# Opening of a layer norm, FFN and attention kernel: batch 1 prepared from the second tile on

## The chip, the cores and the metric

One core of a Trainium2 chip runs the whole kernel. The metric is the device time of one execution in microseconds (us). The five engines run side by side and wait for one another by semaphores only: TensorE (PE, with its weight loads as PEld), VectorE (DVE), ScalarE (ACT), GpSimd (POOL), and SyncE (SP), which issues the DMAs.

## What is computed

```python
x = L0_attn_hidden_states                      # (4, 512, 1024), fp32
xn = _layernorm(x, axis=-1)
s = _L0_attn_ref(xn, Wq, Wk, Wv, Wo)           # 16 heads, rotary, causal
g = _silu(_L0_ffn_ref(xn, ...))
x = x + s * g
...
router_logits = xf @ gate_w.T                  # _L0_ffn_ref, xf = xn as (2048, 1024)
routing = jax.nn.softmax(router_logits, axis=1)        # 8 experts
in_scale = routing @ in_channel_scale
out_scale = routing @ out_channel_scale
out = xf * in_scale @ jnp.sign(weight).T * out_scale + bias
```

## The kernel before

The tokens are 16 tiles of 128 rows, four to each of four batches. The FFN block runs first over all batches (the first 215 us or so), then the attention block. The order of work on each engine is written out by hand; nothing is scheduled by a program. Every fp32 matrix product is made of a high part (`hi`, rounded) and a low part (`lo`, the rest).

The preparation of batch r+1 runs between the FFN matmuls of batch r:

- DVE: `layer_norm(n)` = `ln_stats(n, 2)` (statistics of tiles n and n+1) and `ln_finish(n, 2)` (five small operations after ACT's square root `ln_root`, then the normalisation of both tiles).
- PE: `x_transposes(n)` turns tile n; ACT: `x_high(n)` copies it out in four pieces (hi, and the full value, for two halves); DVE: `x_low(n)` makes the low part. For the tiles of batch 1 and later, `x_transposes(n)` waits for the low parts of tile n-1, since both pass through the same PSUM banks `ff_tr`.
- PE `gate`, ACT `gate_copy`, PE `gate_transposes`, ACT `parts_copy`, DVE `router` with `route_exp` on ACT in its middle, PE `route_transposes`, ACT `route_copy`: the softmax over the experts.
- For each of the eight slices k of 128 channels: PE `in_scale` (one matmul into `ff_tr`), DVE `scale` (writes `xs_full`, two buffers), ACT `xs_high`, POOL `xs_low` (L688). `scale(k)` waits for `xs_low(k-2)`.
- PE `ffn(n, ks)`: four matmuls a slice; at slices 0 and 4 one more for the output scale, which ACT copies (`out_scale`). DVE `z_scale(n)` multiplies, POOL `z_bias(n)` adds the bias.

For batches 1 to 3 the four tiles of batch r+1 are transposed at points spread from the end of `ffn(4r)` to the first slice of `ffn(4r+2)`. For batch 0 the code has a sequence of its own (`if j == 0`), shown with its neighbours here:

Of the kernel before, what the change touches and what calls it, by code (L numbers as in the profile page):

```python
# [21 lines left out]
WARM = (6, 4, 3, 6)  # L22
# [35 lines left out]
def ffn_block(nc, block, io, keep, xn, xn_store, z_store):  # L58

    with ExitStack() as ctx:  # L60
# [147 lines left out]
        def _(pe):  # L208
# [108 lines left out]
            ffn(1, range(KT))  # L317
            for j in range(BATCH):
                more = j + 1 < BATCH
                m = QT * (j + 1)  # L320
                if j == 0:
                    x_transposes(m)
                    ffn(2, range(1))
                    x_transposes(m + 1)
                    ffn(2, range(1, 4))
                    x_transposes(m + 2)
                    ffn(2, range(4, 6))
                    x_transposes(m + 3)
                    ffn(2, range(6, KT))
                    gate(1)  # L330
                    ffn(3, range(2))
                    gate_transposes(1)
                    ffn(3, range(2, 4))
                else:
# [7 lines left out]
                    ffn(QT * j + 1, range(4))  # L342
                    if more:
                        x_transposes(m + 1)
                    ffn(QT * j + 1, range(4, KT))
                    if more:
                        x_transposes(m + 2)
                    ffn(QT * j + 2, range(1))
                    if more:
                        x_transposes(m + 3)  # L350
                    ffn(QT * j + 2, range(1, 4))
                    if more:
                        gate(j + 1)
                    ffn(QT * j + 2, range(4, 6))
                    if more:
                        gate_transposes(j + 1)
                    ffn(QT * j + 2, range(6, KT))
                    ffn(QT * j + 3, range(4))
# [8 lines left out]
        def _(act):  # L367
# [81 lines left out]
            parts_copy(0)  # L449
            route_exp(0)  # L450
            sign(4)
            chan_high(1)
            route_copy(0)
            xs_high(0, range(1))
            xs_high(0, range(1, 2))
            out_scale(0, 0)
            sign(5)
            xs_high(0, range(2, 3))
            sign(6)
            xs_high(0, range(3, 4))  # L460
            sign(7)
            xs_high(0, range(4, KT))
            ln_root(2, 2)
            out_scale(0, 1)
            out_scale(1, 0)
            out_scale(1, 1)
            for j in range(BATCH):
# [3 lines left out]
                if j == 0:  # L471
                    x_high(m)
                    out_scale(2, 0)
                    x_high(m + 1)
                    ln_root(3, 2)
                    out_scale(2, 1)
                    x_high(m + 2)
                    x_high(m + 3)
                    ln_root(4, 2)
                    gate_copy(1)  # L480
                    out_scale(3, 0)
                    parts_copy(1)
                    route_exp(1)
                    out_scale(3, 1)
                    route_copy(1)
                    xs_high(1, range(4))
                    continue
                out_scale(n, 0)
# [38 lines left out]
        def _(dve):  # L527
# [117 lines left out]
            for j in range(BATCH):  # L645
# [17 lines left out]
                if more:  # L663
                    x_low(m)
# [838 lines left out]
```

In the opening ACT also takes the signs of the eight weight rows (`sign(t)`) and copies the two channel tables (`chan_high(c)`; DVE makes their low parts in `chan_low(c)`). `warm(count)` issues matmuls whose result nobody reads.

## Time and profile before

| what | value |
|---|---|
| three runs | 1182.59, 1185.58, 1187.51 us (median 1185.58) |
| profiled execution | 1184.56 us, span 1182.8 us |
| PE busy | 1140.3 us, 96% of the span |
| DVE, ACT, POOL busy | 721.6, 610.7, 420.0 us |
| granted TensorE clock, mean | 0.991 |

The profile shows one execution. Its span is 1.8 us shorter than its time. Times in its views are counted from the start of the span. Busy shares are means over the FFN and the attention, which have different limits, so the change has to be read from the first 90 us.

### The profile page before, as it was taken

The numbers are of one execution on the slowest core, as the hardware profiler recorded it, in microseconds if no ns is written. First come the engines' busy times: TensorE is split into PE (matmuls) and PEld (weight loads), VectorE is DVE, ScalarE is ACT, GpSimd is POOL, SyncE is SP. The second block draws the span as 40 slices with busy tenths as digits, with TensorE's granted clock in tenths as the row PEclk, the third lists the DMA queues.
The fourth block names the chain that finished last, engine by engine and source line by source line (L and its number), as shares of the span: only waits on it lengthen the run. The fifth ranks groups of instructions, "written<-read, shape, count | busy, mean of one in ns | idle before, by whom it ended". The sixth has DMA issues, their size and how long they took to land.

```text
span 1182.8 us, 17759 instructions
## 1 busy us (share of the span) xinstructions
PE 1140.3 (96%) x5699; PEld 949.4 (80%) x5699; DVE 721.6 (61%) x1732; ACT 610.7 (52%) x1285; POOL 420.0 (36%) x253
## 2 busy tenths in 40 slices
PE   5879999999999999999999999999999997999998
PEld 4657777788888888888888888888888886888886
DVE  6466453267776776777776776777776777333132
ACT  6445443155665656646665566655665666322211
POOL 0415527452423533334334242352423533221220
PEclk9889999999999999999999999999999999999999
DMA  9425132302202012022360220202202115555653
GB/s 370 181 89 206 50 118 84 95 7 66 62 9 62 34 46 62 9 66 61 148 213 9 71 62 9 62 13 67 62 9 62 38 60 187 168 178 187 204 176 125
DMA packets 87270, 112.00 MB, mean 95 GB/s; under 512 B 3408, under 2 KB 68944, under 8 KB 86224
## 3 DMA queue, kind: packets, MB, share of 16 engines
q1 hardware_dynamic: 87248, 111.72, 28.7%
q8 instruction: 12, 0.20, 0.1%
q14 instruction: 10, 0.08, 0.0%
HBM read 78.15 MB, written 33.55 MB: 94 GB/s over the span
## 4 chain that ended last, share of the span: by engine, by line
PE 86%; DVE 6%; ACT 4%; POOL 2%; issue 1%; DMA 0%; SPq 0%; DVEq 0%; ACTq 0%; POOLq 0%
PE at_proj L44 17%; PE at_proj L46 17%; PE at_proj L45 17%; PE at_out L987 7%; PE at_pt L974 6%; PE ff_z_ps L287 5%; PE at_score L956 4%; PE at_score L957 3%; PE at_score L44 2%; PE at_score L45 2%; PE at_score L46 2%; POOL ff_xs_lo L688 2%; PE at_proj L941 1%; DVE ff_stats L547 1%; DVE xs_full L609 1%
## 5 line engine op out<-in xcount | busy, mean ns | idle before, releaser
L44 PE MATMUL at_proj<-xn_hi,w_hi 128*128 128x512 f32 x896 | 362.0, 404 | 3.2 <-ACT at_v_t L1092 2.9
L46 PE MATMUL at_proj<-xn_hi,w_lo 128*128 128x512 f32 x896 | 351.0, 392 | 0.0
L45 PE MATMUL at_proj<-xn_lo,w_hi 128*128 128x512 f32 x896 | 349.5, 390 | 0.0
L46 PEld LDWEIGHTS at_proj<-xn_hi,w_lo 128*128 128x128 f32 x896 | 168.2, 188 | 37.3
L44 PEld LDWEIGHTS at_proj<-xn_hi,w_hi 128*128 128x128 f32 x896 | 168.6, 188 | 33.7 <-issue 3.3
L45 PEld LDWEIGHTS at_proj<-xn_lo,w_hi 128*128 128x128 f32 x896 | 169.0, 189 | 30.2
L1351 POOL TENSOR_TENSOR at_turning<-at_turning,rope_table 128x512 f32<-128x512 f32 x64 | 83.0, 1297 | 302.4 <-DVE at_turning L1222 302.4
L1359 POOL TENSOR_TENSOR w_lo<-w_stage,w_hi 128x1024 fp32r<-128x1024 f32 x45 | 114.5, 2558 | 162.7 <-ACT w_hi L1071 162.7
L1109 ACT ACTIVATE at_prob<-at_score,at_neg_max 128x512 f32<-128x512 f32 (+3 forms) x256 | 133.2, 526 | 69.4 <-DVE at_neg_max L1250 69.0
L1118 ACT ACTIVATE at_pt_hi<-at_pt 128x512 fp32r<-128x512 f32 (+1 forms) x192 | 94.1, 524 | 101.8 <-PE at_pt L974 101.0
L1267 DVE TENSOR_TENSOR at_pt_lo<-at_pt,at_pt_hi 128x512 fp32r<-128x512 f32 (+1 forms) x192 | 112.0, 597 | 44.2 <-ACT at_pt_hi L1118 43.2
L1250 DVE CUSTOM_DVE_ANT_0 at_score<-at_score,at_causal 128x512 f32<-128x512 f32 (+3 forms) x256 | 120.7, 514 | 1.0
L974 PE MATMUL at_pt<-ident,at_prob 128*128 128x128 f32 x640 | 93.3, 277 | 5.6 <-DVE at_pt_lo L1267 3.5
L1125 ACT ACTIVATE at_low_half<-at_out 64x512 f32<-64x512 f32 x64 | 37.9, 592 | 103.4 <-PE at_out L987 102.6
L1260 DVE TENSOR_SCALAR at_prob<-at_prob,at_inv_sum 128x256 f32<-128x256 f32 (+3 forms) x256 | 84.5, 393 | 2.3
L287 PE MATMUL ff_z_ps<-sign_t,ff_xs_hi 128*128 128x512 f32 x256 | 84.1, 410 | 1.5 <-POOL ff_xs_lo L688 1.4
L1355 POOL TENSOR_TENSOR at_rotated<-at_turning 128x512 f32<-128x512 f32 x64 | 82.9, 1295 | 7.3 <-POOL at_turning L1351 4.5
L1084 ACT ACTIVATE at_qk<-at_rotated 64x512 fp32r<-64x512 f32 x128 | 80.3, 627 | 7.1 <-POOL at_rotated L1355 5.5
L974 PEld LDWEIGHTS at_pt<-ident,at_prob 128*128 128x128 f32 x640 | 74.5, 143 | 10.9 <-DVE at_pt_lo L1267 4.4
L1367 POOL TENSOR_TENSOR w_lo<-rope_table,w_hi 128x1024 fp32r<-128x1024 f32 x16 | 41.2, 2575 | 115.6 <-ACT w_hi L1138 115.6
L287 PE MATMUL ff_z_ps<-sign_t,ff_xs_lo 128*128 128x512 f32 x256 | 81.7, 401 | 0.0
L956 PE MATMUL at_score<-at_qk 128*128 128x512 f32 (+3 forms) x256 | 80.4, 327 | 0.0
(123 smaller groups left out, 1795.3 us busy)
## 6 DMA issues: line engine op xcount, KB each, us to landing
z_store<-z SPq DMA_DIRECT2D x16, 512.0 KB, 2.6
w_stage<-in_L_attn_Wq_dram SPq DMA_DIRECT2D x16, 512.0 KB, 3.9
w_stage<-in_L_attn_Wk_dram SPq DMA_DIRECT2D x16, 512.0 KB, 5.2
w_stage<-in_L_attn_Wv_dram SPq DMA_DIRECT2D x16, 512.0 KB, 6.2
att_store<-at_att_t SPq DMA_DIRECT2D x32, 256.0 KB, 2.0
rope_table<-att_store SPq DMA_DIRECT2D x16, 512.0 KB, 6.7
z<-_attn_hidden_states_dram SPq DMA_DIRECT2D x16, 512.0 KB, 4.7
at_turning<-z_store SPq DMA_DIRECT2D x16, 512.0 KB, 6.0
```

The source lines that it names most:

```text
L44: pe.matmul(out, sh, mh, start=first, stop=False)
L45: pe.matmul(out, sh, ml, start=False, stop=False)
L46: return pe.matmul(out, sl, mh, start=False, stop=final)
L287: last = pe.matmul(z_ps[n % 2][:, o, :], part[:, k, tok], keep["sign_t"][:, k, o * HALF:(o + 1) * HALF], start=(k == 0 and part is xs_hi), ...
L956: pe.matmul(out, q, k_hh[parity][h][:, 0:width], start=True, stop=False)
L974: last = pe.transpose(pt_ps[u % 2][:, dst:dst + P], prob[h][:, src:src + P], keep["ident"][:])
L1109: last = act.activation(prob[h][:, P_COL[t]:P_COL[t] + width], score_ps[bank][:, col:col + width], ACT.Exp, scale=-1.0, bias=neg_max[h][:, ...
L1118: act.activation(pt_hi[h][:, 512 * u:512 * u + PT_WIDTH[u]], pt_ps[u % 2][:, 0:PT_WIDTH[u]], ACT.Copy).then_inc(pt_high, 1)
L1250: last = dve.tensor_tensor_reduce(out=row, in0=row, in1=causal[:, (QT - 1 - t) * P:SEQ], scale=-1.0, scalar=FAR, op0=ALU.add, op1=ALU.min, ...
L1260: last = dve.tensor_scalar(part, part, inv_sum[h][:, t:t + 1], None, ALU.mult)
L1267: dve.tensor_tensor(pt_lo[h][:, cols], pt_ps[u % 2][:, 0:PT_WIDTH[u]], raw(pt_hi[h][:, cols]), ALU.subtract).then_inc(pt_ready, 1)
L1359: pool.tensor_tensor(w_lo[m][:], w_raw[m], raw(w_hi[m][:]), ALU.subtract).then_inc(w_ready[m], 1)
```

## The change

PE: for batch 0 the special sequence is dropped, and batch 1's first tile (tile 4) is transposed right behind `ffn(0)`, tile 5 in the middle of `ffn(1)`, tile 6 ahead of `ffn(2)` and tile 7 behind its first slice, as in later batches. Seven of 19 warm matmuls go. DVE: the statistics of tiles 4 and 5 are taken one tile at a time between scales, and their square root and normalisation come between scales too; the statistics of tiles 6 and 7 come before `z_scale(0)`. ACT: a small `exp_table()` puts the load of the exponential's table ahead of `gate_copy(0)`; `sign(0)` and `chan_high(0)` move ahead of `x_high(0)`, the other signs move by some places, `chan_high(1)` comes earlier, and `ln_root(2)` moves from behind the eighth `xs_high` to behind the fifth. `chan_low(1)` moves ahead of the scales.

```diff
@@ PE
-            warm(WARM[1])
             pe.wait_ge(tables, 1)
             gate(0, (0, 1))
             gate(0, (2, 3))
+            warm(WARM[1])
+            gate_transposes(0)
             warm(WARM[2])
-            gate_transposes(0)
-            warm(WARM[3])
...
-            ffn(1, range(KT))
             for j in range(BATCH):
...
                 if j == 0:
                     x_transposes(m)
-                    ffn(2, range(1))
-                    x_transposes(m + 1)
-                    ffn(2, range(1, 4))
-                    x_transposes(m + 2)
-                    ffn(2, range(4, 6))
-                    x_transposes(m + 3)
-                    ffn(2, range(6, KT))
-                    gate(1)
-                    ffn(3, range(2))
-                    gate_transposes(1)
-                    ffn(3, range(2, 4))
...
+                ffn(QT * j + 1, range(4))
+                if more:
+                    x_transposes(m + 1)
+                ffn(QT * j + 1, range(4, KT))
+                if more:
+                    x_transposes(m + 2)
+                ffn(QT * j + 2, range(1))
+                if more:
+                    x_transposes(m + 3)
+                ffn(QT * j + 2, range(1, 4))
@@ ACT
+            def exp_table():
+
+                act.activation(route_e[0:1, 0, 0:1], ln[0:1, 1, 0:1], ACT.Exp)
...
             ln_root(0, 2)
+            sign(0)
+            chan_high(0)
             x_high(0)
             ln_root(1, 2)
             x_high(1)
-            chan_high(0)
-            sign(0)
+            sign(1)
             x_high(2)
             x_high(3)
-            sign(1)
-            sign(2)
-            sign(3)
+            exp_table()
+            chan_high(1)
             gate_copy(0)
             parts_copy(0)
             route_exp(0)
...
+            xs_high(0, range(4, 5))
+            ln_root(2, 2)
+            xs_high(0, range(5, 6))
@@ DVE
-            ln_stats(4, 2)
-            scale(0, range(4, KT))
-            ln_finish(4, 2)
+            scale(0, range(3))
+            ln_tile(4, 0)
+            scale(0, range(3, 4))
+            ln_moments(ln_tile(4, 1), 2)
+            scale(0, range(4, 5))
+            scale(0, range(5, 6))
+            ln_inverse(2)
+            scale(0, range(6, 7))
+            ln_apply(4, 0)
+            scale(0, range(7, KT))
+            ln_apply(4, 1)
+            ln_stats(6, 2)
             z_scale(0)
```

On PE, from the last slice of `ffn(0)` on, the program before had this (L279 is the output scale's matmul, L287 the FFN's, L219 the transposes; the left-out rows are the same two L287 rows, slice by slice):

```order
L287 MATMUL ff_z_ps<-sign_t,ff_xs_hi 128x512 x2
L287 MATMUL ff_z_ps<-sign_t,ff_xs_lo 128x512 x2
L279 MATMUL ff_osc_ps<-chan_out,ff_route_t 128x512
...
L287 MATMUL ff_z_ps<-sign_t,ff_xs_lo 128x512 x2
L219 MATMUL ff_tr<-ident,w_stage 128x128 x8
L279 MATMUL ff_osc_ps<-chan_out,ff_route_t 128x512
```

The changed program has this from the same slice on:

```order
L287 MATMUL ff_z_ps<-sign_t,ff_xs_hi 128x512 x2
L287 MATMUL ff_z_ps<-sign_t,ff_xs_lo 128x512 x2
L219 MATMUL ff_tr<-ident,w_stage 128x128 x8
L279 MATMUL ff_osc_ps<-chan_out,ff_route_t 128x512
```

The eight transposes of tile 4 have moved ahead of the eight slices of `ffn(1)`.

On DVE, behind the router of batch 0, the program before had this (L609 is `scale`, L547 to L552 the statistics, L564 the normalisation, L617 `chan_low(1)`):

```order
L609 TENSOR_TENSOR xs_full<-ff_tr,xn_full 128x512 x2
L617 TENSOR_TENSOR chan_out<-z,chan_out 64x1024
L609 TENSOR_TENSOR xs_full<-ff_tr,xn_full 128x512 x2
L547 BN_STATS ff_stats<-w_stage 128x6 x4
L550 BN_AGGR ff_moments<-ff_stats 128x2 x2
L552 TENSOR_SCALAR ff_ln<-ff_moments 128x2
L609 TENSOR_TENSOR xs_full<-ff_tr,xn_full 128x512 x4
...
L564 TENSOR_SCALAR w_stage<-w_stage,ff_moments,ff_ln 128x1024 x2
L624 TENSOR_TENSOR z<-ff_z_ps,ff_out_sc 128x1024
```

The changed program has this there (L598 is `scale`, L522 to L530 the statistics, L548 the normalisation, L606 `chan_low(1)`; the rows left out are four more of the five small operations that begin with L540, and then the statistics of tiles 6 and 7):

```order
L606 TENSOR_TENSOR chan_out<-z,chan_out 64x1024
L598 TENSOR_TENSOR xs_full<-ff_tr,xn_full 128x512 x3
L522 BN_STATS ff_stats<-w_stage 128x6 x2
L598 TENSOR_TENSOR xs_full<-ff_tr,xn_full 128x512
L522 BN_STATS ff_stats<-w_stage 128x6 x2
L528 BN_AGGR ff_moments<-ff_stats 128x2 x2
L530 TENSOR_SCALAR ff_ln<-ff_moments 128x2
L598 TENSOR_TENSOR xs_full<-ff_tr,xn_full 128x512 x2
L540 RECIPROCAL ff_ln<-ff_ln 128x2
...
L598 TENSOR_TENSOR xs_full<-ff_tr,xn_full 128x512
L548 TENSOR_SCALAR w_stage<-w_stage,ff_moments,ff_ln 128x1024
L598 TENSOR_TENSOR xs_full<-ff_tr,xn_full 128x512
L548 TENSOR_SCALAR w_stage<-w_stage,ff_moments,ff_ln 128x1024
```

The two normalisations stood behind all scales and now stand around the eighth; the two table operands of `chan_low(1)` are read before the first scale.

## Rows read from the trace of the kernel before

**Rows 1.** The page: the span and the engines' busy time.

```profile
span 1182.8 us, 17759 instructions
PE 1140.3 (96%) x5699; PEld 949.4 (80%) x5699; DVE 721.6 (61%) x1732; ACT 610.7 (52%) x1285; POOL 420.0 (36%) x253
```

**Rows 2.** Windows: length; busy PE, PEld, DVE, ACT, POOL; clock, DMA share, GB/s.

```profile
30.17:86.58 56.41, 47.28 (x188) 32.76 (x188) 32.35 (x72) 24.79 (x44) 18.26 (x11) 0.88 0.36 137
86.58:131.21 44.63, 43.37 (x201) 32.19 (x202) 27.37 (x58) 21.93 (x40) 19.66 (x12) 1.00 0.39 154
131.21:175.70 44.49, 43.24 (x202) 32.05 (x200) 22.18 (x44) 21.78 (x40) 19.65 (x12) 1.00 0.27 83
66.10:71.60 5.50, 5.50 (x17) 4.61 (x18) 1.65 (x3) 2.56 (x5) 0.00 (x0) 0.51 0.31 98
```

**Rows 3.** Timeline of PE: start, duration, what, and the idle time before it.

```profile
46.04 0.73 PE L287 MATMUL ff_z_ps<-sign_t,ff_xs_hi 128*128 128x512 f32 x2
...
55.04 1.04 PE L219 MATMUL ff_tr<-ident,w_stage 128*128 128x128 f32 x8
...
66.10 1.94 PE L219 MATMUL ff_tr<-ident,x_tiles 128*128 128x128 f32 x8 [4.05 <-DVE xn_lo L578]
...
105.38 1.03 PE L219 MATMUL ff_tr<-ident,w_stage 128*128 128x128 f32 x8
...
131.21 0.39 PE L262 MATMUL ff_tr<-ff_route_t,chan_in 128*128 128x512 f32 x1
```

**Rows 4.** Timeline of DVE from 56 us to 65 us.

```profile
56.86 0.69 DVE L578 TENSOR_TENSOR xn_lo<-ff_tr,xn_hi 128x512 fp32r<-128x512 f32 x1 [7.02 <-ACT xn_full L394]
...
58.45 1.21 DVE L624 TENSOR_TENSOR z<-ff_z_ps,ff_out_sc 128x1024 f32<-128x1024 f32 x1
59.58 2.46 DVE L547 BATCH_NORM_STATS2 ff_stats<-x_tiles 128x6 f32<-128x512 f32 x4
...
62.83 0.17 DVE L557 RECIPROCAL ff_ln<-ff_ln 128x2 f32<-128x2 f32 x1 [0.27 <-ACT ff_ln L378]
...
63.82 1.53 DVE L564 TENSOR_SCALAR x_tiles<-x_tiles,ff_moments,ff_ln 128x1024 f32<-128x1024 f32 x2
```

**Rows 5.** Timelines of ACT and DVE in the first 28 us.

```profile
10.77 0.60 ACT L391 ACTIVATE xn_hi<-ff_tr 128x512 fp32r<-128x512 f32 x1 [3.11 <-PE ff_tr L219]
...
13.29 0.20 ACT L378 ACTIVATE ff_ln<-ff_ln 128x2 f32<-128x2 f32 x1 [0.46 <-DVE ff_ln L552]
...
26.04 1.28 ACT L411 ACT_TABLE_LOAD   x1
27.33 0.23 ACT L411 ACTIVATE ff_route_e<-ff_route 128x32 f32<-128x32 f32 x1
...
20.03 1.22 DVE L617 TENSOR_TENSOR chan_in<-z,chan_in 64x1024 fp32r<-64x1024 f32 x1
...
26.50 0.19 DVE L588 TENSOR_TENSOR ff_route<-ff_route,ff_route_m 128x32 f32<-128x32 f32 x1
```

**Rows 6.** DMA issues between 3.0 and 4.0 us: count, size, us to landing.

```profile
weight_rows<-in_L_ffn_weight_dram SPq DMA_DIRECT2D x1, 512.0 KB, 7.2
z<-fn_in_channel_scale_dram SPq DMA_DIRECT2D x1, 512.0 KB, 8.0
```

**Rows 7.** The chain that ended last, one slice k of the scales.

```profile
39.20 0.70 DVE xs_full L609
39.92 0.64 ACT ff_xs_hi L428
40.64 1.30 POOL ff_xs_lo L688
```

**Rows 8.** One line of POOL (ns min/median/max), and rows of the attention.

```profile
L688 POOL TENSOR_TENSOR ff_xs_lo<-xs_full,ff_xs_hi x32: 1272/1288/2135, 32.2 to 187.4; 128x512 fp32r<-128x512 f32 x32
...
301.32 1.27 DVE L1260 TENSOR_SCALAR at_prob<-at_prob,at_inv_sum 128x256 f32<-128x256 f32 x4
...
977.29 2.41 POOL L1363 TENSOR_TENSOR xn_lo<-w_stage,xn_hi 128x1024 fp32r<-128x1024 f32 x1
978.74 4.15 DVE L1260 TENSOR_SCALAR at_prob<-at_prob,at_inv_sum 128x256 f32<-128x256 f32 x4
```

More of the change, by code:

```diff
@@ L21 @@
 STEPS = 2 * 2 * PAIRS
-WARM = (6, 4, 3, 6)
+WARM = (6, 2, 4)
 MASK = -1.0e9 / 8.0
@@ L341, in _ @@
                     ffn(QT * j, range(7, KT))
[L342 to L358, printed above, removed]
+                ffn(QT * j + 1, range(4))
[8 more added lines that the diff above has]
+                ffn(QT * j + 2, range(1, 4))
+                if more:
+                    gate(j + 1)
+                ffn(QT * j + 2, range(4, 6))
+                if more:
+                    gate_transposes(j + 1)
+                ffn(QT * j + 2, range(6, KT))
+                ffn(QT * j + 3, range(4))
                 if more:
@@ L450, in _ @@
             route_exp(0)
+            sign(2)
+            sign(3)
+            route_copy(0)
+            xs_high(0, range(2))
             sign(4)
[L452 to L455, printed above, removed]
+            xs_high(0, range(2, 3))
             out_scale(0, 0)
+            xs_high(0, range(3, 4))
             sign(5)
-            xs_high(0, range(2, 3))
+            xs_high(0, range(4, 5))
+            ln_root(2, 2)
+            xs_high(0, range(5, 6))
             sign(6)
-            xs_high(0, range(3, 4))
+            xs_high(0, range(6, 7))
             sign(7)
-            xs_high(0, range(4, KT))
-            ln_root(2, 2)
+            xs_high(0, range(7, KT))
             out_scale(0, 1)
-            out_scale(1, 0)
-            out_scale(1, 1)
             for j in range(BATCH):
@@ L470, in _ @@
                 m = n + QT
[L471 to L488, printed above, removed]
-                xs_high(j, range(4, KT))
-                out_scale(n, 1)
+                if j >= 1:
+                    out_scale(n, 0)
+                    xs_high(j, range(4, KT))
+                    out_scale(n, 1)
                 if not more:
@@ L540, in gate_w_low, with ln_tile, ln_moments @@
                                   raw(keep["gate_t"][:, :, 0:EXPERTS]), ALU.subtract).then_inc(tables, 1)
-            def ln_stats(n, count):
-                for t in range(count):
-                    slot = X_SLOT[n + t]
-                    dve.wait_ge(x_in[slot], 16 * X_SLOT[:n + t + 1].count(slot))
-                    for h in range(2):
-                        last = dve.bn_stats(stats[:, t, h, :], x_tile[n + t][:, h * HALF:(h + 1) * HALF])
+            def ln_tile(n, t):
+                slot = X_SLOT[n + t]
+                dve.wait_ge(x_in[slot], 16 * X_SLOT[:n + t + 1].count(slot))
+                for h in range(2):
+                    last = dve.bn_stats(stats[:, t, h, :], x_tile[n + t][:, h * HALF:(h + 1) * HALF])
+                return last
+            def ln_moments(last, count):
                 then(last)
@@ L552, in ln_stats, with ln_inverse @@
                 dve.tensor_scalar(ln[:, 0, 0:count], moments[:, 0:count, 1], LN_EPS, None, ALU.add).then_inc(ln_var, 1)
-            def ln_finish(n, count):
+            def ln_stats(n, count):
+                for t in range(count):
+                    last = ln_tile(n, t)
+                ln_moments(last, count)
+            def ln_inverse(count):
                 roots[0] += 1
```

38 lines of the change are left out of this document (16 added, 22 removed).

## The prediction

> **What bounds the kernel now.** The page comes first [rows 1]: PE is busy for 96% of the span, so work on the other engines counts only where PE stands still for it. The second view is a table of windows, cut at the first input scale matmul of batches 0, 1, 2 and 3 (30.17, 86.58, 131.21, 175.70 us) [rows 2]. All three windows hold the same kinds of work, one batch each. The second and third last 44.63 and 44.49 us with PE busy for 43.3 and at a granted clock of 1.00. The first lasts 56.41 us at 0.88. So batch 0 costs about 11.8 us more than a batch in the settled rhythm, and that is all that a new order of its work can give back.
>
> The third view, PE's timeline, says where the 11.8 us lie [rows 3]. `ffn(0)`'s last slice starts at 46.04; until there PE follows the slower chain of the scales. Then `ffn(1)` runs without a gap, and tile 4 is transposed only at 55.04. At 66.10 PE has stood idle for 4.05 us, because the low parts of tile 5 were late. DVE's timeline says why [rows 4]: DVE was idle for 7.02 us until 56.86, waiting for tile 4 to come out of PE, and then had `z_scale(1)`, the statistics of tiles 6 and 7 (2.46 us), their five small operations and their normalisation (1.53 us) in front of tile 5's low part. DVE had nothing to do, then too much. Behind PE's idle time the granted clock is 0.51 for 5.5 us [rows 2], the lower of its two levels (1.2 of 2.4 GHz), so the PE work there took twice its time: some 2.7 us more. Idle time and low clock together are 6.8 of the 11.8 us; small waits and the scales' pace in `ffn(0)` are the rest.
>
> **The change, part by part.** I follow it along the path.
>
> *Before the router.* `sign(0)` and `chan_high(0)` now stand ahead of `x_high(0)`, and their data must have landed. The weight row is issued at 3.07 us and needs 7.2, the table at 3.56 and needs 8.0 [rows 6]: 10.3 and 11.6 us. The table's copy takes 0.95, so `x_high(0)` begins at 12.57 instead of 10.77 [rows 5]. Its four copies take 1.93, so the root of tiles 2 and 3 starts at 14.50 instead of 13.29: DVE is 1.2 us late with their normalisation. Against this stand two things that leave the path: the 1.22 us of `chan_low(0)` between low parts [rows 5], and the idle time on ACT. Carried through (DVE 0.6 us for each half's low part, ACT 0.48 for each copy, transposes of tile 3 behind tile 1's low part), the last low part ends at 22.7, about 0.1 us later than before. I count a loss of 0.1.
>
> *The exponential's table.* The load stood between the router's sum and its exponential: it ran from 26.04 to 27.33 [rows 5], while DVE had the operand ready at 26.69 (26.50 + 0.19) [rows 5]. Now the exponential starts 0.6 us earlier. The load itself falls into the time between tile 3's last copy (about 21.8) and `gate_copy(0)` (24.8), where ACT needs 1.28 + 0.2 + 0.95 for the load, the dummy and `chan_high(1)` and ends at 24.25; were that cover gone, up to 1.3 us would be back. The trace shows the exponential right behind the load, so 0.6 is all of it. The Trainium skill, ScalarE: Activation LUTs, What ACT_TABLE_LOAD costs, adds a drain of about 1.38 us to every switch; by it the gain here would be 0.6 + 1.4 = 2.0. No such drain is visible before or behind this row, so the trace decides against it and it gets no chance of its own. In sum the first input scale matmul starts at 30.17 + 0.1 - 0.6 = 29.66 us. The seven warm matmuls that go cost nothing on the path: PE waits for others around them. What they may do to the clock is a rival below.
>
> *The scales of batch 0.* One slice takes 0.72 us from DVE to ACT, 0.72 from ACT to POOL and 1.30 on POOL [rows 7]; `scale(k)` needs `xs_low(k-2)`. Starting the first scale at 30.17: POOL does slice 0 from 31.71 to 33.00 and slice 1 to 34.25. It is not held up by `chan_low(1)` now, which has left. Before, slice 0 took 2135 ns against a median of 1288 [rows 8], a gain of 0.85. Then the new work on DVE sets in:
>
> - scale 2 at 33.05, one tile's statistics (half of 2.46), scale 3 at 34.84 (0.6 late), the other statistics and their two small steps (1.6), scale 4 at 37.14 (1.3 late), scale 5 at 37.75;
> - ACT: `xs_high` 4 at 37.86, then the square root's table load (1.28, the size of the load in [rows 5]), so `xs_high` 5 at 39.79, again 1.3 late; POOL does slice 4 until 39.86 and slice 5 from 40.50 to 41.79;
> - DVE: the five small operations take 0.99 (62.83 to 63.82 in [rows 4]) behind the root, scale 6 at 40.91; then the normalisations (0.77 each) around scale 7.
>
> The last two steps meet POOL. In the attention four such scalings in SBUF took 4.15 us where POOL's 2.41 us subtraction was under way [rows 8]; without POOL the same four take 1.27. And POOL's first slice was stretched just while `chan_low(1)` ran on DVE. So I take it that the normalisations (810 ns for 1024 columns) and `xs_low` exclude each other: the first waits until 41.79 and ends at 42.6, slice 6 runs from 42.6 to 43.89, the second normalisation takes 43.89 to 44.7, and slice 7 runs from 44.7 to 45.99. The Trainium skill, SBUF — State Buffer, Who interferes with whom, says it as a rule: VectorE in a two-port mode and GpSimd lock each other out for the whole instruction. By the rule the sum is this one; without it slice 7 would end at 45.10. `ffn(0)`'s last slice then starts at 46.04 (45.15 without), exactly where it did. All that was gained ahead has gone into preparing tiles 4 to 7. If DVE were blocked at neither place and ACT's load were hidden too, the last slice could start about 2.5 us earlier; that is the upper bound.
>
> *Tile 4 and after.* The last slice's four matmuls take 0.94, so tile 4 is transposed at 46.98 instead of 55.04 [rows 3]. Its operand has long been normalised. `ffn(1)`'s first half (0.24 + 4 x 0.94) and the transposes (0.8) bring tile 5 to 51.76. What tile 5 waits for, the low parts of tile 4, starts 1.1 and 2.1 us behind the transposes, at 48.1 and 49.1, with nothing in front of it: covered by `ffn(1)`, 2 us to spare. The statistics of tiles 6 and 7 (2.9 us with their small steps) and `z_scale(0)` (1.2) fit between 44.7 and 48.8. From tile 5 on the order on every engine is that of batch 1, where the same point is 105.38 and the next batch's first input scale 131.21 [rows 3]: 25.83 us. So batch 1's scales start at 51.76 + 25.83 = 77.6 us instead of 86.58. POOL and SP keep their orders; their stores and loads are released earlier with the tiles.
>
> **The sum**: 9.0 us. Checked against the windows: 77.6 - 29.66 = 47.9 us for batch 0, 3.3 above the 44.6 of the others, which is the slow pace of `ffn(0)`. Everything behind 86.58 (three batches and the attention) keeps its order and moves as a whole. The profiled execution took 1184.56 us (span 1182.8 and 1.8 around it), so 1184.56 - 9.0 = 1175.6 us. It lies 1.0 under the median of three.
>
> **Rivals.**
> 1. *DVE and POOL don't collide*, or a table load and the statistics cost less than taken. `ffn(0)` ends 0.9 us earlier: 1174.7; with every cover perfect (2.5) 1173.1, and never under 1184.56 - 11.8 - 0.5 = 1172.3, since batch 0 can't beat the settled rhythm. For it: the collision needs an overlap of some tenths. Chance 0.18.
> 2. *The clock falls earlier.* With fewer warm matmuls, and tiles 2 and 3 transposed 1.2 us later, PE has gaps of 1.8 and 1.5 us between 14 and 20 us. At the lower level PE's work takes twice its time [rows 2]; behind the last low part some 2 us of gate matmuls lie on the path, and `ffn(0)` may be 1 us late besides: 2 to 3 us lost, 1178.1. Against it: the gaps before were only a little shorter, and the clock stayed up. Chance 0.15.
> 3. *The wait moves.* If tile 6 or 7's normalisation or a root behind `out_scale(1, 0)` on ACT were late, PE would stand again at tile 6 for up to 4 us, as at 66.10, with part of the low clock behind it: 5 of the 9 us return, 1180.6. My count has 3 us to spare there, so 0.08.
> 4. *Slower than before.* The clock falls in `ffn(0)` and doesn't come back, because PE there has short gaps at each slice. At the lower level each microsecond of such a stretch holds half a microsecond of work, so 9.0 us are eaten after 18 us of it in PE bound work, beyond those of before; 30 us would give 1190.6. Before, the clock came back in the same stretch though PE waited there too. Chance 0.03.
>
> My forecast has the remaining 0.56.
>
> **Numbers.** The forecast 1175.6; the range 1171.5 to 1180 takes in rivals 1 and 2, the lower bound of 1172.3 and some noise of a median of runs that lie 4.9 us apart. About 0.5%, 6 us, is what this measurement can tell from no change. Faster by more (under 1179.7): forecast and rivals 1 and 2, less a tail, 0.87. Within 0.5%: mostly rival 3, 0.10. Slower: 0.03.
>
> **What would show it.** Tile 4 transposed at about 47 us and tile 5 at 52; no idle time of over 1.5 us on PE from 46 on, and a clock of 1.00 there; first input scale matmul at 29.7, that of batch 1 at 77.6. On DVE no 7 us of idle time; a normalisation or an `xs_low` stretched to over 1.4 us near 42 to 45. ACT's first `x_high` at 12.6. A low clock between 14 and 25 us speaks for rival 2, PE idle before tile 6 for rival 3. The prediction is wrong if batch 0's window isn't shorter than 51 us, or if a later window is longer than 44.7.

## The result

The changed kernel took 1178.69 us (median of 16 runs), the kernel before 1184.89 (16 runs on the same chip, 1182.59 to 1187.51). Fifteen of the changed kernel's runs lie between 1176.53 and 1182.3; the sixteenth took 1270.32 us in a slower state, with a mean granted clock of 0.846, and is left out of the ratio. The ratio is 0.995, with a 95% interval of 0.9941 to 0.9959: 6 us faster where 9.0 were forecast. The profiled execution took 1177.60 us against 1184.56, a gain of 7.0.

Windows of the changed kernel, cut at the first input scale matmul of batches 0, 1, 2 and 3, and two short ones at low clock (columns as in [rows 2]):

```profile
29.41:78.61 49.20, 45.02 (x189) 32.72 (x190) 33.43 (x71) 25.49 (x45) 17.59 (x11) 0.90 0.38 148
78.61:123.10 44.49, 43.23 (x202) 32.04 (x200) 27.39 (x58) 21.98 (x41) 19.68 (x12) 1.00 0.42 166
123.10:167.59 44.49, 43.25 (x201) 32.06 (x200) 22.19 (x44) 21.78 (x40) 19.63 (x12) 1.00 0.27 83
44.80:48.20 3.40, 3.19 (x8) 2.38 (x9) 3.37 (x7) 0.76 (x2) 1.65 (x2) 0.50 0.00 0
225.60:229.10 3.50, 3.50 (x10) 2.75 (x9) 1.37 (x2) 0.55 (x1) 0.00 (x0) 0.51 0.00 0
```

Batch 0's window fell from 56.41 to 49.20 us, and the later ones are what they were. But 47.9 was forecast. A stretch at the lower clock inside `ffn(0)` is new (44.8 to 48.2), and so is one at the start of the attention. They are not the only ones: the clock is also low from 31.4 to 38.0 us, as it was from 30.8 to 37.6 in the kernel before, where the prediction counted only the 5.5 us at 66.10. Such a stretch, of some 6.8 us or more, stands at the start of the scales of batch 0 in every profile of this case.

Timeline of PE in the changed kernel, the rows that answer to [rows 3]:

```profile
29.41 0.71 PE L262 MATMUL ff_tr<-ff_route_t,chan_in 128*128 128x512 f32 x2 [0.73 <-DVE chan_out L606]
...
42.05 0.73 PE L287 MATMUL ff_z_ps<-sign_t,ff_xs_hi 128*128 128x512 f32 x2 [0.82 <-POOL ff_xs_lo L676]
...
45.01 1.22 PE L287 MATMUL ff_z_ps<-sign_t,ff_xs_hi 128*128 128x512 f32 x2 [1.76 <-POOL ff_xs_lo L676]
...
46.88 1.05 PE L287 MATMUL ff_z_ps<-sign_t,ff_xs_hi 128*128 128x512 f32 x2
...
48.42 1.03 PE L219 MATMUL ff_tr<-ident,w_stage 128*128 128x128 f32 x8
...
53.26 1.04 PE L219 MATMUL ff_tr<-ident,w_stage 128*128 128x128 f32 x8
...
60.71 0.63 PE L219 MATMUL ff_tr<-ident,x_tiles 128*128 128x128 f32 x4 [0.38 <-DVE xn_lo L567]
...
78.61 0.39 PE L262 MATMUL ff_tr<-ff_route_t,chan_in 128*128 128x512 f32 x1
```

The 4.05 us wait at 66.10 and the low clock behind it are gone; tile 7's halves wait 0.38 and 0.26 us. (At 29.41 ACT's copy of the routing weights, ended at 29.31, was awaited as well as `chan_low(1)`, ended at 29.33, so that move cost nothing here.) What is new is the wait of 1.76 us at 45.01 for the low part of slice 6, and the last two slices at half speed behind it.

Timeline of DVE in the changed kernel around the five small operations (L530 closes the statistics of tiles 4 and 5, L540 to L545 are `ln_inverse(2)`, L598 `scale`, L548 the normalisation):

```profile
36.85 0.51 DVE L530 TENSOR_SCALAR ff_ln<-ff_moments 128x2 f32<-128x2 f32 x1
...
40.16 0.17 DVE L540 RECIPROCAL ff_ln<-ff_ln 128x2 f32<-128x2 f32 x1 [1.62 <-ACT ff_ln L365]
40.37 0.16 DVE L542 TENSOR_TENSOR ff_ln<-ff_ln 128x2 f32<-128x2 f32 x1
40.56 0.16 DVE L543 TENSOR_TENSOR ff_ln<-ff_ln 128x2 f32<-128x2 f32 x1
40.76 1.27 DVE L544 TENSOR_SCALAR ff_ln<-ff_ln 128x2 f32<-128x2 f32 x1
42.06 0.16 DVE L545 TENSOR_TENSOR ff_ln<-ff_ln 128x2 f32<-128x2 f32 x1
42.25 0.69 DVE L598 TENSOR_TENSOR xs_full<-ff_tr,xn_full 128x512 f32<-128x512 f32 x1
42.86 0.80 DVE L548 TENSOR_SCALAR w_stage<-w_stage,ff_moments,ff_ln 128x1024 f32<-128x1024 f32 x1
```

Timeline of POOL in the same stretch:

```profile
40.73 1.27 POOL L676 TENSOR_TENSOR ff_xs_lo<-xs_full,ff_xs_hi 128x512 fp32r<-128x512 f32 x1 [0.76 <-ACT ff_xs_hi L419]
43.69 1.27 POOL L676 TENSOR_TENSOR ff_xs_lo<-xs_full,ff_xs_hi 128x512 fp32r<-128x512 f32 x1 [1.69 <-ACT ff_xs_hi L419]
45.15 1.50 POOL L676 TENSOR_TENSOR ff_xs_lo<-xs_full,ff_xs_hi 128x512 fp32r<-128x512 f32 x1 [0.20 <-ACT ff_xs_hi L419]
```

The operation at 40.76 handles two numbers in each row. Its like takes 0.16 to 0.17 us, this one took 1.27, and it ends 0.03 us behind the `xs_low` of slice 5, which began 0.03 us ahead of it. Scale 6 stands behind it, so POOL then waits 1.69 us for slice 6, and PE 1.76. The operation at 36.85 is held too, for 0.34 us: it ends at 37.36, and the `xs_low` of slice 3 ran until 37.33.

Timeline of ACT in the changed kernel, where the opening's moves show (against [rows 5]):

```profile
10.07 1.06 ACT L357 ACTIVATE sign_t<-weight_rows 128x1024 fp32r<-128x1024 f32 x1 [1.92 <-DMA weight_rows<-in_L_ffn_weight_dram]
11.36 1.06 ACT L393 ACTIVATE chan_in<-z 128x1024 fp32r<-128x1024 f32 x1 [0.22 <-DMA z<-fn_in_channel_scale_dram]
12.32 0.58 ACT L378 ACTIVATE xn_hi<-ff_tr 128x512 fp32r<-128x512 f32 x1
...
21.71 1.28 ACT L402 ACT_TABLE_LOAD   x1
23.00 0.20 ACT L402 ACTIVATE ff_route_e<-ff_ln 1x1 f32<-1x1 f32 x1
...
26.56 0.23 ACT L398 ACTIVATE ff_route_e<-ff_route 128x32 f32<-128x32 f32 x1 [0.71 <-DVE ff_route L577]
```

`x_high(0)` waits for the landed data, as predicted (12.57 there, 12.32 here), and the exponential has no load ahead of it.

### The profile page after: what moved, and what is told of

It is laid out like the page before. It is cut to its first block, busy times and chain, and to the rows that moved or that the text cites. A ratio compares the mean times of both kernels' runs of the same rounds, so it can differ in the third digit from the quotient of the medians.

```text
span 1175.8 us, 17746 instructions
## 1 busy us (share of the span) xinstructions
PE 1137.9 (97%) x5692; PEld 949.1 (81%) x5692; DVE 723.9 (62%) x1732; ACT 611.3 (52%) x1286; POOL 419.4 (36%) x253
## 4 chain that ended last, share of the span: by engine, by line
PE 87%; DVE 5%; ACT 3%; POOL 2%; issue 1%; DMA 1%; SPq 0%; DVEq 0%; ACTq 0%; POOLq 0%
PE at_proj L44 17%; PE at_proj L46 17%; PE at_proj L45 17%; PE at_out L975 7%; PE ff_z_ps L287 6%; PE at_pt L962 6%; PE at_score L944 4%; PE at_score L945 3%; PE at_score L44 2%; PE at_score L46 2%; PE at_score L45 2%; POOL ff_xs_lo L676 1%; PE at_proj L929 1%; DVE xs_full L598 1%; ACT xn_hi L378 1%
## 5 line engine op out<-in xcount | busy, mean ns | idle before, releaser
L287 PE MATMUL ff_z_ps<-sign_t,ff_xs_hi 128*128 128x512 f32 x256 | 84.3, 411 | 3.4 <-POOL ff_xs_lo L676 3.4
L287 PE MATMUL ff_z_ps<-sign_t,ff_xs_lo 128*128 128x512 f32 x256 | 82.0, 402 | 0.0
```

Of the source, the lines that this page charges most:

```text
L287: last = pe.matmul(z_ps[n % 2][:, o, :], part[:, k, tok], keep["sign_t"][:, k, o * HALF:(o + 1) * HALF], start=(k == 0 and part is xs_hi), ...
```

## The experiments

Since the first transposes start anywhere from 9.4 to 10.5 us, with the landing of the input, one profile is compared with another by distances. The table has, from each kernel's one profile, the distance from the first transposes to the first input scale matmul (opening), from there to tile 4's transposes (scales), from there to batch 1's first input scale matmul (batch), and from there to the end of the span (rest); then its median and its ratio to the kernel before on the same chip.

| kernel | opening | scales | batch | rest | median us | ratio (95%) |
|---|---|---|---|---|---|---|
| before | 20.53 | 24.87 | 31.54 | 1096.2 | 1184.89 | 1 |
| changed | 19.27 | 19.01 | 30.19 | 1097.2 | 1178.69 | 0.995 (0.9941 to 0.9959) |
| a0_changed_again | 21.25 * | 19.48 | 30.37 | 1097.5 | 1178.89 | 0.9946 (0.9933 to 0.9959) |
| e1_order_only | 20.55 | 17.87 | 30.91 | 1097.8 | 1177.93 | 0.995 (0.9937 to 0.9963) |
| e2_inverse_behind | 21.19 * | 19.16 | 31.77 | 1096.5 | 1179.12 | 0.9964 (0.9951 to 0.9976) |
| e3_root_late | 19.95 | 17.37 | 30.27 | 1096.7 | 1175.33 | 0.9928 (0.9914 to 0.9942) |
| e3_again | 20.26 | 17.67 | 30.27 | 1094.8 | 1175.17 | 0.992 (0.9901 to 0.9939) |
| e8_root_between | 21.10 * | 16.96 | 30.28 | 1096.5 | 1176.64 | 0.9932 (0.9918 to 0.9945) |
| e7_best_order | 18.77 | 16.61 | 30.27 | 1095.2 | 1174.03 | 0.9912 (0.9893 to 0.993) |
| e4_attn_fill | 20.93 * | 19.22 | 30.22 | 1095.7 | 1177.93 | 0.995 (0.9937 to 0.9963) |
| e5_warm_back | 20.31 | 19.19 | 31.35 | 1094.7 | 1178.28 | 0.9948 (0.9936 to 0.9961) |
| e6_no_exp_table | 22.33 * | 19.35 | 30.22 | 1097.2 | 1180.25 | 0.9954 (0.9939 to 0.9969) |

A star marks a profile with a low clock that begins between 16.7 and 19.4 us.

### e1_order_only: the new order of batch 1's preparation alone

The PE order of the change stays; ACT, the warm matmuls and the scales are as before, except that the statistics of tiles 6 and 7 stand ahead of `z_scale(0)`.

```diff
-            scale(0, range(3))
-            ln_tile(4, 0)
...
-            ln_apply(4, 1)
+            scale(0, range(2))
+            chan_low(1)
+            scale(0, range(2, 4))
+            ln_stats(4, 2)
+            scale(0, range(4, KT))
+            ln_finish(4, 2)
```

> Only the new order of batch 1's preparation on PE, ACT and DVE, with the statistics of tiles 6 and 7 ahead of z_scale(0); tables, signs, warm matmuls and the work between batch 0's scales stand as in the kernel before. Theory A (all of the gain is the order behind ffn(0); what the other edits win ahead of it, the scales lose again to the statistics, the root's table load and the exclusion of VectorE and GpSimd): the last slice of ffn(0) at 46.0 us as before, tile 4 transposed at 48.1, when its normalisation is done, batch 1's first input scale at 78.3, ratio to before 0.993 to 0.996, the same as the full change. Rival B (the other edits carry some of the gain): 79.5 us or later and a ratio of 0.997 or more.

Tile 4 was transposed at 47.86 and batch 1's first input scale came at 78.77, near the 48.1 and 78.3 expected. The ratio is that of the whole change, 0.995. So the new order of the tiles brings the gain and the remaining edits together bring nothing that can be told. In the profiles they are not nothing: they shorten the opening by 1.28 us (20.55 to 19.27), lengthen the scales by 1.14 (17.87 to 19.01) and shorten the column "batch" by 0.72 (30.91 to 30.19).

### e2_inverse_behind: the five small operations behind scale 6

```diff
-            ln_inverse(2)
             scale(0, range(6, 7))
+            ln_inverse(2)
             ln_apply(4, 0)
```

> The changed kernel with one edit: the five small operations of the normalisation stand behind scale 6 instead of ahead of it. Theory A (scale 6 is late because the small TENSOR_SCALAR on 128x2 elements, 1.27 us instead of 0.17, and the root stand in front of it): scale 6 starts at about 40.1 instead of 42.25 us, the idle time of 1.76 us on PE before slice 6 is under 0.5, tile 4 is transposed at 46.5 to 47.7 instead of 48.42, and the time is 0.7 to 1.9 us under the changed kernel's. Rival B (GpSimd sets the pace, whatever stands on VectorE): tile 4 still at 48.2 or later, same time.

The expected gain did not come: tile 4 was transposed at 49.88, later than in the changed kernel, and the ratio is 0.9964. By these two numbers the rival had it, but the rows show another reason than its own. Timeline of DVE in e2_inverse_behind:

```profile
41.71 0.69 DVE L598 TENSOR_TENSOR xs_full<-ff_tr,xn_full 128x512 f32<-128x512 f32 x1 [1.54 <-POOL ff_xs_lo L676]
42.32 0.15 DVE L540 RECIPROCAL ff_ln<-ff_ln 128x2 f32<-128x2 f32 x1
42.51 1.14 DVE L542 TENSOR_TENSOR ff_ln<-ff_ln 128x2 f32<-128x2 f32 x1
43.68 0.16 DVE L543 TENSOR_TENSOR ff_ln<-ff_ln 128x2 f32<-128x2 f32 x1
43.88 1.26 DVE L544 TENSOR_SCALAR ff_ln<-ff_ln 128x2 f32<-128x2 f32 x1
...
46.10 0.68 DVE L598 TENSOR_TENSOR xs_full<-ff_tr,xn_full 128x512 f32<-128x512 f32 x1
```

And of POOL there:

```profile
42.35 1.27 POOL L676 TENSOR_TENSOR ff_xs_lo<-xs_full,ff_xs_hi 128x512 fp32r<-128x512 f32 x1 [0.75 <-ACT ff_xs_hi L419]
43.82 1.29 POOL L676 TENSOR_TENSOR ff_xs_lo<-xs_full,ff_xs_hi 128x512 fp32r<-128x512 f32 x1 [0.20 <-ACT ff_xs_hi L419]
47.52 1.27 POOL L676 TENSOR_TENSOR ff_xs_lo<-xs_full,ff_xs_hi 128x512 fp32r<-128x512 f32 x1 [2.41 <-ACT ff_xs_hi L419]
```

Scale 6 is no longer late (10.99 us behind the first input scale matmul, against 12.84 in the changed kernel), and PE's wait before slice 6 is 0.29 us, as theory A had it. But the small operations now meet two `xs_low` instead of one and each time one of them waits to its end (42.51 + 1.14 = 43.65 against 42.35 + 1.27 = 43.62; 43.88 + 1.26 = 45.14 against 43.82 + 1.29 = 45.11). So scale 7, with the normalisation of tile 4 also in front of it, is late instead, and POOL waits 2.41 us for it. The miss agrees with the mechanism and shows that moving the operations by one scale only moves the wait.

### e3_root_late and e8_root_between: small operations behind all scales

In e3_root_late the second root (ACT), the small operations and the normalisation of tiles 4 and 5 stand behind the eighth scale, and the statistics of tiles 6 and 7 fill their places. e8_root_between is the same with the root, and so the table load, back between the copies of slices 4 and 5.

```diff
             scale(0, range(5, 6))
-            ln_inverse(2)
+            ln_tile(6, 0)
             scale(0, range(6, 7))
-            ln_apply(4, 0)
+            then(ln_tile(6, 1))
             scale(0, range(7, KT))
-            ln_apply(4, 1)
-            ln_stats(6, 2)
+            ln_finish(4, 2)
```

> The changed kernel with square root, small operations and normalisation of tiles 4 and 5 behind all eight scales, and the statistics of tiles 6 and 7 between scales in their place (bn_stats alone, which read one operand). Theory A: no xs_low over 1.35 us and no small operation over 0.2, xs_high 5 about 1.4 us earlier, the last slice of ffn(0) at 44 to 44.5 instead of 46.88; but tile 4 then waits for its normalisation, at 46.0 to 46.5 instead of 48.42; 1.5 to 2.3 us under the changed kernel. Rival B: the last slice of ffn(0) stays at 46 or later, since the chain of scale, copy and subtraction of slices sets it alone.

> e3 with one edit: the square root of tiles 4 and 5, with its table load, stands between xs_high 4 and 5 again; the five small operations and the normalisation stay behind all scales. It tells the load on ScalarE from the blocked small operations on VectorE. Theory A1 (the blocked operations were the larger part of what e3 gained): last slice of ffn(0) at about 45.5, no wait for the normalisation, tile 4 transposed at 46.0 to 46.9, time within 0.5 us of e3. Rival A2 (the load was): last slice at 46.5 or later and 1 us or more above e3.

e3_root_late reached 1175.33 us, ratio 0.9928. Timeline of DVE in e3_root_late:

```profile
40.24 0.69 DVE L599 TENSOR_TENSOR xs_full<-ff_tr,xn_full 128x512 f32<-128x512 f32 x1 [0.35 <-POOL ff_xs_lo L678]
40.85 1.28 DVE L522 BATCH_NORM_STATS2 ff_stats<-x_tiles 128x6 f32<-128x512 f32 x2
42.16 0.69 DVE L599 TENSOR_TENSOR xs_full<-ff_tr,xn_full 128x512 f32<-128x512 f32 x1
45.07 0.17 DVE L541 RECIPROCAL ff_ln<-ff_ln 128x2 f32<-128x2 f32 x1 [2.21 <-ACT ff_ln L365]
...
46.06 1.53 DVE L549 TENSOR_SCALAR w_stage<-w_stage,ff_moments,ff_ln 128x1024 f32<-128x1024 f32 x2
```

The scales leave with the statistics between them, and these are not stretched: the two at 40.85 take the usual 0.64 us each. None of the five small operations is held, since POOL has finished when they run. The last slice starts at 44.92 and tile 4 is transposed at 46.92, each 0.4 us behind the range that was expected. The price is that tile 4's transposes now wait for their normalised operand (0.81 us on PE), and still the stage is 1.6 us shorter than in the changed kernel (17.37 against 19.01).

Timeline of DVE in e8_root_between, where the root comes early but the small operations stand behind the scales:

```profile
42.63 1.27 DVE L522 BATCH_NORM_STATS2 ff_stats<-x_tiles 128x6 f32<-128x512 f32 x2
44.07 0.69 DVE L599 TENSOR_TENSOR xs_full<-ff_tr,xn_full 128x512 f32<-128x512 f32 x1 [0.17 <-POOL ff_xs_lo L678]
44.68 0.15 DVE L541 RECIPROCAL ff_ln<-ff_ln 128x2 f32<-128x2 f32 x1
44.87 0.57 DVE L543 TENSOR_TENSOR ff_ln<-ff_ln 128x2 f32<-128x2 f32 x1
45.48 0.16 DVE L544 TENSOR_TENSOR ff_ln<-ff_ln 128x2 f32<-128x2 f32 x1
45.67 1.23 DVE L545 TENSOR_SCALAR ff_ln<-ff_ln 128x2 f32<-128x2 f32 x1
```

And of POOL there:

```profile
44.13 1.29 POOL L678 TENSOR_TENSOR ff_xs_lo<-xs_full,ff_xs_hi 128x512 fp32r<-128x512 f32 x1 [0.19 <-ACT ff_xs_hi L419]
45.60 1.28 POOL L678 TENSOR_TENSOR ff_xs_lo<-xs_full,ff_xs_hi 128x512 fp32r<-128x512 f32 x1 [0.17 <-ACT ff_xs_hi L419]
```

Two of the small operations are held here too (0.57 and 1.23 us), but no scale stands behind them, and PE at tile 4 waits for nothing. The reciprocal at 44.68 runs at its usual pace under POOL's operation. The stage takes 16.96 us, and the ratio of 0.9932 can't be told from e3_root_late's. The last slice started at 46.93, which taken alone is the sign of rival A2; but the first input scale matmul was 1.49 us later than in e3_root_late, and counted from there the last slice is 0.52 later (15.89 against 15.37), where the changed kernel is 2.10 later (17.47). So most of what made the changed kernel's stage long was that scales stood behind the small operations, and the table load on ACT between two copies accounts for 0.5 us at most by these two profiles. Both kernels also moved the normalisations behind the scales. No run separates these; in the changed kernel's rows one of them stretched the `xs_low` of slice 7 by 0.2 us (1.50 at 45.15).

### e7_best_order and e3_again: the order that the experiments point to

e7_best_order is e3_root_late with `sign(0)` and `chan_high(0)` taken back from ahead of `x_high(0)`, the signs in ACT's pauses, and the statistics one tile between every two scales.

```diff
             ln_root(0, 2)
-            sign(0)
-            chan_high(0)
             x_high(0)
             ln_root(1, 2)
             x_high(1)
-            sign(1)
+            chan_high(0)
             x_high(2)
...
```

> The order of e3_root_late (the second root, the five small operations and the normalisation of tiles 4 and 5 behind all of batch 0's scales), with two further moves. ScalarE: sign(0) and chan_high(0) stand behind x_high(1), so that x_high(0) need not wait for the sign and channel data, and the other signs fill ScalarE's pauses in the opening and between the scaled copies. VectorE: the statistics of tiles 4 to 7 stand one tile between every two scales. Theory A (a term of the prediction: x_high(0) waits for data that lands late, 12.32 here against 10.77 before, and the small operations stall ahead of scale 6): the first input scale comes about 1.1 us earlier behind the first transposes than in e3_root_late (19.95 us behind them there, so 18.8 to 18.9), the last slice stays paced by GpSimd, tile 4 is transposed at 44.5 to 45.5, and the ratio to the kernel before is about 0.991, 1.5 to 2.5 us under e3_root_late. Rival (the opening is bound by the weights, the exponential or the router and not by x_high(0)): first input scale 19.7 to 20.2 us behind the first transposes and the ratio within 0.001 of e3_root_late's. Second rival (the moved statistics or signs hold back a scaled copy): the slices stand more than 2.6 us apart on GpSimd with waits for ScalarE or VectorE, and the ratio is above e3_root_late's.

> The kernel of e3_root_late on this job's chip, for the comparison with e7_best_order. Both theories: ratio 0.9915 to 0.994, as in its first run (0.9928); a ratio of 0.995 or more would say that its lead over the changed kernel (0.995) was not resolved.

Both ran on one chip: 1174.03 and 1175.17 us. Timeline of ACT in e7_best_order:

```profile
11.25 0.60 ACT L378 ACTIVATE xn_hi<-ff_tr 128x512 fp32r<-128x512 f32 x1 [3.11 <-PE ff_tr L219]
```

`x_high(0)` starts 1.13 us behind the first transposes (10.12), where in e3_again it starts 2.95 behind them (12.76 and 9.81) and in the changed kernel 2.18 (12.32 and 10.14). The opening is 1.49 us shorter than in e3_again and the stage of the scales 1.06; the first transposes came 0.31 later, so batch 1's first scale is 2.24 us earlier (75.77 and 78.01). The opening of 18.77 us and tile 4 at 45.50 are as expected. The medians are 1.14 apart, less than the 1.5 to 2.5 expected, with intervals that overlap, so the timing alone doesn't settle this last step. Against the changed kernel it does: 0.9893 to 0.993 lies wholly under 0.9941, and under the 0.9933 at which the interval of a0_changed_again begins. It is the fastest version found, 11 us under the kernel before.

### a0, e5, e4, e6: the clock and the table

a0_changed_again is the changed kernel once more, on the chip of e5, e6 and e8; e5_warm_back has the old 19 warm matmuls (`WARM = (6, 4, 3, 6)`); e4_attn_fill adds ten matmuls that nobody reads behind the attention's first step; e6_no_exp_table takes `exp_table()` out again.

```diff
+            step(0, 0, 0)
+            fill(10)
+            step(0, 1, 1)
...
-            exp_table()
             chan_high(1)
```

> The changed kernel unchanged, as the reference of the same chip for the three runs below. Ratio to before 0.994 to 0.996.

> The changed kernel with the warm matmuls of before (19 instead of 12, at their old places). Theory C (in part of the executions the clock falls near 19 us, as in the profiles of e2 and e4, since PE does less there; each fall costs about 1.6 us up to the first input scale): median 0.5 to 1.5 us under the changed kernel's on the same chip, no lower clock before 29 us, highest run lower. Rival D (warm matmuls are without effect, the fall comes from the phase alone): same median within 0.4 us, and falls near 19 us stay possible.

> The changed kernel with ten unread 512-column matmuls behind the attention's first step, in the 2.9 us in which PE waits there. The profile of the changed kernel shows a granted clock at the lower level for 3.4 us right behind this gap, which the kernel before does not show. Theory C (part of the 9 us is lost here, by the phase at which the gap falls): the clock stays at 1.00 up to 980 us, and the time is 1.0 to 1.7 us under the changed kernel's. Rival D: the lower clock there is an accident of the profiled execution, absent from most runs; the median moves by less than 0.4 us.

> The changed kernel without the early load of the exponential's table; the load then stands between the router's sum and the exponential. Theory A (the gain ahead of the scales is kept only in part): first input scale 0.7 us later relative to the first transposes (20.0 instead of 19.3 us), tile 4 later by the same 0.7, time up by 0.5 to 0.9 us. Rival: it costs 2 us, a load and a drain behind it; or nothing, since the scales absorb it.

A window of a0_changed_again from 16.7 us on (columns as in [rows 2]):

```profile
16.70:23.50 6.80, 5.97 (x27) 4.83 (x28) 5.89 (x11) 6.12 (x11) 0.00 (x0) 0.50 1.03 409
```

The same window of e5_warm_back:

```profile
16.70:23.50 6.80, 5.26 (x40) 4.29 (x41) 6.34 (x10) 6.45 (x13) 0.00 (x0) 1.00 1.03 410
```

The fall of the clock before the router exists: in a0_changed_again tile 2 was transposed at 16.89 behind 2.04 us of idle PE, at the lower level. Seven of the profiles have the changed kernel's opening up to the router. Without the early fall it takes 19.27, 19.95 and 20.26 us, with it 20.93, 21.10, 21.19 and 21.25. Part of that is not the clock. `x_high(0)` waits for the sign and channel data, and it started 2.18, 2.90 and 2.95 us behind the first transposes in the three without the fall and 3.06 to 3.18 behind them in the four with it. From `x_high(0)` on the opening takes 17.05 to 17.31 us without the fall and 17.76 to 18.19 with it, so the fall costs about 0.8 us (17.99 against 17.15 on average).

The start of `x_high(0)` also sorts all twelve profiles: where it came 1.12 to 3.03 us behind the first transposes (seven profiles) the clock stayed up, where it came 3.06 to 3.28 behind them (five) it fell. That points to the late data, for which the change makes `x_high(0)` wait, and e7_best_order, which takes the wait away, had no fall in its profile. But 3.03 and 3.06 are close, and no run moved the landing of the data alone, so the cause is argued and not shown. e5_warm_back had no fall there either, at 3.03 us; its median is 0.61 us under the changed kernel's with the same ratio, and its one profile has 6.8 us of low clock at 44.7. So whether the warm matmuls prevent anything stays open.

e4_attn_fill closed the idle time at the attention's start. Timelines of PE there, in the changed kernel:

```profile
225.00 0.47 PE L44 MATMUL at_proj<-xn_hi,w_hi 128*128 128x512 f32 x1 [2.88 <-ACT at_v_t L1080]
```

and in e4_attn_fill:

```profile
226.46 0.47 PE L44 MATMUL at_proj<-xn_hi,w_hi 128*128 128x512 f32 x1 [0.64 <-ACT at_v_t L1090]
```

The clock stayed up there. The ratio is 0.995, that of the changed kernel, and the opening happened to have the early fall, so the timing decides nothing. The column "rest" of the table says more: the seven profiles with a low clock near 225 us (changed, a0, e1, e2, e3_root_late, e8, e6) have a mean rest of 1097.1, the five without 1095.3. These 1.8 us are not the price of that stretch alone, since there are further stretches behind 970 us. Added up in 2 us windows from batch 1's first scale to the end, the low clock is about 8.7 us in the kernel before and 11.4 in the changed one. The three profiles with the least of it (e5, e3_again, e7: 4.1 to 5.2 us) have the shortest rests, 1094.7 to 1095.2; the five with the most (e3_root_late, changed, e6, e1, a0: 10.7 to 14.4 us) have 1096.7 to 1097.8. By that, as an estimate, a stretch of 3.4 us costs some 1.1 us.

e6_no_exp_table took 1180.25 us against 1178.89 of a0_changed_again on the same chip, 1.4 more, with overlapping intervals. Its opening was 1.08 us longer, both with the early fall. Timeline of ACT in e6_no_exp_table:

```profile
28.30 0.22 ACT L389 ACTIVATE ff_parts<-ff_small 128x64 f32<-128x64 f32 x1 [0.51 <-PE ff_small L239]
28.54 1.28 ACT L398 ACT_TABLE_LOAD   x1
29.83 0.23 ACT L398 ACTIVATE ff_route_e<-ff_route 128x32 f32<-128x32 f32 x1
```

The load is back ahead of the exponential, and the exponential starts 1.53 us behind `parts_copy(0)`, where in a0_changed_again it starts 0.93 behind it (28.20 and 27.27). So the move is worth 0.60 us, as forecast. The rest of the 1.08 is `x_high(0)`, 0.22 later behind the first transposes, and small differences on either side of the load. The timing's 1.4 is not resolved. By the Trainium skill, ScalarE: Activation LUTs, What ACT_TABLE_LOAD costs, the estimate would have been 2.0 us for this move. The rows show 1.28 us for the load and the exponential right behind it, so no drain is seen here either.

## Why the prediction was right in kind and its gain 2 to 3 us too large

The forecast of 1175.6 stands against 1178.69 (a gain of 9.0 against 6.2 by the medians and 7.0 by the profiles); the time lies in the range, and the change is faster by just over 0.5%. By the prediction's own test (batch 0's window under 51 us, none of the later ones over 44.7) it holds with 49.20 and 44.49. Its mechanism was right and one term was mis-sized. In the profiled execution the steps add up like this:

- **The opening**, first scale at 29.66 forecast, 29.41 measured, 0.25 better. The load left the path with 0.60 as forecast, and from `x_high(0)` to the first scale 17.09 us were forecast and 17.09 measured. The 0.25 are the landed table (`x_high(0)` at 12.32 instead of 12.57). The early fall of the clock was rival 2, with 0.15; of the changed kernel's two profiles one has it, and in the opening it is worth about 0.8 us, where the rival had 2 to 3 in all.
- **The scales of batch 0**, the term that failed: from the first scale to tile 4's transposes 17.32 us were forecast (46.98 - 29.66) and 19.01 measured, 1.69 worse. The step was: "the five small operations take 0.99 (62.83 to 63.82 in [rows 4]) behind the root, scale 6 at 40.91". I had applied the exclusion of DVE and POOL to the normalisations of 1024 columns and priced the small operations from a place where POOL stood idle. They took 2.09 us (40.16 to 42.25), since one of them was held for a whole `xs_low`, and the root before them was 0.24 later than counted; so scale 6 left at 42.25, which is 1.34 late. The first normalisation, expected to be held until 41.79, was not; it came into POOL's pause, and only the second one was held (1.32 us at 44.18). The last slice started at 46.88 instead of 46.04. That these two lie so close is in part luck: the prediction had 0.9 us in it for the holds of the normalisations (46.04 against 45.15), most of which did not come, and nothing for the hold that did.
- Of the 1.44 us by which tile 4 was late in all (48.42 against 46.98), 0.66 is POOL, which ended slice 7 at 46.65 instead of 45.99. The other 0.78 is the lower clock from 44.8 to 48.2: it kept PE on slice 6 some 0.18 us beyond that, and the last slice's four matmuls took 1.54 instead of 0.94. It came behind PE's 1.76 us wait, and not by chance: all six profiles in which PE waits 1.76 us or more in the scales (changed, a0, e2, e4, e5, e6) have a low clock right behind the wait, and the six in which the longest wait there is under 1 us have none in the scales beyond the early stretch that every profile has. So the clock's share follows from the held operation. A clock of 1.00 from 46 us on, which the prediction named as a sign, was wrong.
- **Tile 4 and after**: tile 5 came 4.84 behind tile 4 (4.78 forecast) and batch 1's first scale 25.35 behind tile 5 (25.83 taken from batch 1): 0.48 better, mostly since the first interval between two tiles' transposes is 4.86 us here and 5.29 in batch 1 (105.38 to 110.67 in the profile before). No wait moved to tile 6: rival 3 did not occur.
- **Sum**: 0.25 - 1.69 - 0.06 + 0.48 = -1.02. At batch 1's first scale the gain is 7.97 instead of 9.0, and 8.08 at the attention's start (233.08 to 225.00).
- **Everything behind**, which was to move as a whole, was off by 1.1 us in this profile: the gain at the end is 7.0, with a stretch of low clock at 225.7 us that the profile before did not have. The idle time ahead of it was the same (2.88 and 2.86 us). The median's gain of 6.2 is lower still. Here the mean clock of every execution helps: the changed kernel's two at 0.994 took 1176.53 and 1177.63 us, its two at 0.988 1178.52 and 1182.3; e2_inverse_behind's two at 0.994 took 1176.57 and 1176.96, its three at 0.987 1182.02 to 1182.77. So the time of an execution follows how long the clock was low in it. Which stretches these were in executions without a profile is not known, and why the clock falls at the same place in one execution and not in another stays open.

e2_inverse_behind, e3_root_late and e8_root_between together show the failed term: the hold meets the small operations wherever they run beside an `xs_low`, and costs the scales time only where a scale stands behind them. The row from the attention on which the prediction based its exclusion fits too, though it spans two POOL operations (977.29 to 979.70 and 979.66 to 982.08 us) and not only the one shown in [rows 8]. e1_order_only shows that the gain comes from the tiles' new order alone. Rival 1 (no collision, 1174.7) did not happen, and rival 4 did not either.

## What to carry to other kernels

Price every operation that is moved between the links of a chain at the place where it will stand, not where it stood: an operation of 0.16 us that can be locked out by another engine's instruction costs up to that instruction's whole length, here 1.27 us, and all five stood ahead of the scale that POOL, and then PE, waited for. Fill the pauses of such a chain with operations that the other engine can't hold (here the statistics), and put the others behind its last link. When the median differs from the sum by 1 or 2 us, look where the granted clock fell in each profile before looking for a further wait.

## What the runs showed of the hardware

- A DVE operation on 128x2 elements whose operands lie in SBUF waited to the end of POOL's two-input operation in SBUF: 1.27 and 0.51 (changed), 1.14 and 1.26 (e2_inverse_behind), 0.57 and 1.23 us (e8_root_between) instead of 0.16 or 0.17, for TENSOR_TENSOR and TENSOR_SCALAR. Each ended 0.02 to 0.03 us behind POOL's. The Trainium skill, SBUF — State Buffer, Who interferes with whom, says that VectorE in a two-port mode and GpSimd lock each other out "for the whole instruction", and that a VectorE instruction with two SBUF inputs contends with a GpSimd instruction that reads SBUF. It names no least size. The rows of TENSOR_SCALAR and of TENSOR_TENSOR agree. RECIPROCAL (0.15 at 44.68, under POOL's operation from 44.13 on) and BATCH_NORM_STATS2 (0.64 each at 42.63, under the one from 42.66 on) ran at their usual pace in e8_root_between, and so did the 128x512 scaling with one operand in PSUM in the changed kernel (0.67 at 34.63, under the one from 34.26 to 35.54).
- The granted clock fell behind waits of PE of some 2 us: 2.04 at 16.89 (a0_changed_again), 1.76 at 45.01 and 2.88 at 225.00 (changed). The same wait did not always bring it down: the wait of 2.85 to 2.88 us at the attention's start stands in eleven profiles, and the clock fell behind it in seven of them, not in the kernel before (2.86 at 233.08), e3_again, e5_warm_back and e7_best_order. In the opening of e3_root_late a wait of 2.00 us ahead of 16.52 was not followed by a fall.
